# The skip term as matrix products in a fused Mamba and mixture-of-experts kernel, its gate on VectorE, and one product moved to GpSimd

## What is computed

```
xc = silu(causal_conv4(xn @ W_in[:, :512]) + conv_b)        # 512 rows x 512 channels
dt = softplus((xc @ W_x)[:, :64] @ W_dt + b_dt);  z = xn @ W_in[:, 512:]
h[l] = exp(dt[l] * A) * h[l-1] + (dt[l] * xc[l]) * B[l]     # 16 states per channel
y    = sum over the 16 states of h * C  +  D_skip * xc      # the skip term
x    = x + ga * ((y * silu(z)) @ W_out)                     # the gate, the output projection
```

## Time and profile before

| | us |
|---|---|
| median of three runs (1579.13 to 1584.12) | 1581.85 |
| the profiled execution | 1585.96 |
| its span, first to last instruction | 1584.2 |
| outside the span | 1.8 |
| first scan starts | 66.6 |
| period of a sequence in the middle (730.26 to 860.05) | 129.8 |
| end of the last scan | 1105.3 |

### The profile page before, as it was taken

One profiled execution on the slowest core, in us unless ns is written; L12 is line 12 of the kernel. 1 busy time (PEld: TensorE's weight loads), 2 busy tenths in 40 slices (PEclk: granted clock), 3 DMA queues, 4 the chain that ended last, 5 costly groups with the idle time before them and its releaser, 6 DMA issues.

```text
span 1584.2 us, 25969 instructions
## 1 busy us (share of the span) xinstructions
PE 1336.4 (84%) x7986; PEld 1086.1 (69%) x7986; DVE 1219.8 (77%) x2155; ACT 783.9 (49%) x1376; POOL 1044.8 (66%) x942
## 2 busy tenths in 40 slices
PE   3676876876867998788798798869799999999998
PEld 1254564565655776657666576768689989999997
DVE  3798999899899889989989988987355545555554
ACT  2666867767766776786787677666000000000000
POOL 2486778798889789889899878986414352122222
PEclk7787899889889889999999999999899999999999
DMA  6212121223134333244333332674967788766663
GB/s 223 74 48 77 50 54 55 75 92 88 48 100 122 123 114 126 79 143 141 104 107 104 105 111 100 180 235 136 332 179 197 209 241 221 208 194 200 198 193 85
DMA packets 129073, 216.60 MB, mean 137 GB/s; under 512 B 17805, under 2 KB 74649, under 8 KB 128809
## 3 DMA queue, kind: packets, MB, share of 16 engines
q1 hardware_dynamic: 110104, 184.12, 38.0%
q0 software_dynamic: 16064, 27.62, 7.0%
q10 hardware_dynamic: 2768, 3.21, 0.7%
HBM read 178.60 MB, written 37.22 MB: 136 GB/s over the span
## 4 chain that ended last, share of the span: by engine, by line
PE 45%; DVE 18%; POOL 14%; issue 10%; ACT 8%; DMA 3%; SPq 1%; POOLq 0%; DVEq 0%; ACTq 0%
PE psum L1665 13%; PE psum L1681 13%; POOL dBu L873 10%; DVE w_sb L1965 9%; PE psum L1477 6%; DVE y L1976 3%; PE psum L1486 2%; ACT psum L1124 2%; ACT hc L1108 2%; PE psum L1621 1%; PE psum L1466 1%; PE psum L1634 1%; DVE w_sb L1946 1%; DVE xc L1946 1%; DMA w_sb<-in_W 1%
## 5 line engine op out<-in xcount | busy, mean ns | idle before, releaser
L873 POOL TENSOR_TENSOR dBu<-w_sb,brep 128x512 f32<-128x512 f32 x512 | 645.6, 1325 | 42.1 <-issue 18.1
L1965 DVE TENSOR_TENSOR_SCAN w_sb<-psum,dBu 128x512 f32<-128x512 f32 x512 | 611.6, 1210 | 77.5 <-ACT psum L1124 54.6
L1477 PE MATMUL psum<-ident,w_sb 128*128 128x128 f32 x2048 | 316.8, 305 | 116.8 <-DVE y L1976 66.8
L1124 ACT ACTIVATE psum<-w_sb,aneg 128x512 f32<-128x512 f32 x512 | 347.4, 692 | 134.3 <-DVE w_sb L1965 131.4
L1477 PEld LDWEIGHTS psum<-ident,w_sb 128*128 128x128 f32 x2048 | 262.0, 157 | 192.5 <-DVE y L1976 106.1
L860 POOL DMA_INDIRECT out<-dBu,token x59 | 92.2, 1563 | 305.4 <-DMA out<-dBu,token 200.8
L1108 ACT ACTIVATE hc<-psum,ct 128x512 f32<-128x512 f32 x256 | 174.7, 682 | 124.8 <-PE psum L1477 96.6
L1486 PE MATMUL psum<-ident,hc 128*128 128x128 f32 x1024 | 173.7, 302 | 36.2 <-ACT hc L1108 28.8
L1486 PEld LDWEIGHTS psum<-ident,hc 128*128 128x128 f32 x1024 | 135.0, 156 | 81.9 <-ACT hc L1108 53.8
L1976 DVE SCALAR_TENSOR_TENSOR y<-psum,ct,y 128x512 f32<-128x512 f32 x240 | 174.5, 727 | 13.6 <-PE psum L1477 13.1
L1665 PE MATMUL psum<-xn,expert_pieces 128*128 128x128 f32 x928 | 111.4, 280 | 8.2 <-issue 8.2
(11 more groups left out here) (265 smaller groups left out, 1745.1 us busy)
## 6 DMA issues: line engine op xcount, KB each, us to landing
brep<-b_d SPq DMA_DIRECT2D x128, 256.0 KB, 5.4
win<-in_W SPq DMA_DIRECT2D x30, 1024.0 KB
expert_pieces<-in_W SPq DMA_DIRECT2D x29, 1024.0 KB
expert_pieces<-in_W SPq DMA_DIRECT2D x42, 512.0 KB, 5.3
dBu<-rows_d SPq DMA_DIRECT2D x35, 257.0 KB
w_sb<-in_W SPq DMA_DIRECT2D x8, 1024.0 KB
xg<-rows_d SPq DMA_DIRECT2D x22, 257.0 KB, 2.8
h_d<-hmod SPq DMA_DIRECT2D x8, 512.0 KB, 3.5
```

The lines of the kernel that those rows point to most:

```text
L873: nc.gpsimd.tensor_tensor(dBu[:, i % RING, :], u[p][:, c, :], brep[:, s % 4, :], ALU.mult).then_inc(s_dBu, 1)
L1124: nc.scalar.activation(dA[:, i % DA_RING, :], dt[p][:, c, :], ACT.Exp, scale=aneg[:, c, s:s + 1]).then_inc(s_dA, 1)
L1477: last = nc.tensor.transpose(T[:, i // DT, c * P:(c + 1) * P], hs[s % 2][:, c, i * P:(i + 1) * P], ident[:, :])
L1965: nc.vector.tensor_tensor_scan(hs[s % 2][:, c, :], dA[:, i % DA_RING, :], dBu[:, (n * UNITS + i) % RING, :], 0.0, ALU.mult, ALU.add).then_ ...
```

## The change

**The skip term.** Four 128x128 diagonal matrices of D_skip (`skip_diagonals`) are made once by VectorE in the prologue. After each `y_t`, TensorE adds 16 products of such a matrix and xc into `YT` (`add_skip`). VectorE's `o_gate` then multiplies `YT` by silu(z) in four instructions; GpSimd's `gate` is gone.

**dt times x.** The product leaves VectorE's state 13 and is made by GpSimd in four chunks after its inputs of state 15; each chunk releases its own first `dBu` of the next sequence.

**ScalarE.** In each state `decays` of unit 0 stands alone, followed by the work that stood behind unit 1 in states 0, 8, 9, 12, 13 and 14; in state 11 `softplus_in(0)` moves behind unit 2's decay, and in state 8 `o_norm` is issued in one piece ahead of unit 3's.

**The end.** The two buffers of W1 trade places, SP issues W1 of tile 12 before its rows and the rows of tiles 13, 14 and 16 after two more loads, `first(BEGIN)` is split in two around the last `add_up`, `y_t` and `add_skip`, and ScalarE applies scale and bias to the first rows of tile 13 and bias and ReLU to tile 12 in place of VectorE.

```diff
@@ -148,7 +148,7 @@
-        w1_of = [win[:, :, :], wp[:, 0:2, :]]
+        w1_of = [wp[:, 1:3, :], win[:, :, :]]
@@ -532,7 +534,7 @@
-                        if (slot_of(g) >= 3) == (t == BEGIN) and slot_of(g) != 2:
+                        if slot_of(g) in ((1, 2) if t == BEGIN else (3, 4)):
@@ -623,18 +627,20 @@
+                late_w1(BEGIN)
...
-                late_w1(BEGIN)
-                for t in (BEGIN + 1, BEGIN + 2, BEGIN + 4):
-                    late_rows(t)
...
+                for t in (BEGIN + 1, BEGIN + 2, BEGIN + 4):
+                    late_rows(t)
...
+                first_columns(BEGIN + 1)
+                sp.wait_ge(s_tr, NB * UNITS - TI)
+                all_w2(6)
...
-                all_w2(6)
@@ -715,12 +721,6 @@
-            def gate(n, p, chunks=range(CH)):
-                pool.wait_ge(s_zs, n + 1)
-                for c in chunks:
-                    pool.wait_ge(s_g, n * CH + c + 1)
-                    nc.gpsimd.tensor_tensor(gT[:, c, :], gT[:, c, :], sz[p][:, c, :], ALU.mult).then_inc(s_gate, 1)
-
@@ -860,13 +860,18 @@
 
+            def dt_x(n, p):
+                pool.wait_ge(s_dt, n)
+                for c in range(CH):
+                    nc.gpsimd.tensor_tensor(u[p][:, c, :], dt[p][:, c, :], xc[p][:, c, :], ALU.mult).then_inc(s_u, 1)
+
             def inputs(n, p, s, has_before, chunks=range(CH)):
...
                     i = n * UNITS + s * CH + c
-                    if s == 0 and has_before and c == 0:
-                        pool.wait_ge(s_u, n)
+                    if s == 0 and has_before:
+                        pool.wait_ge(s_u, (n - 1) * CH + c + 1)
                     if s == 0 and not has_before and c % 2 == 0:
@@ -937,12 +936,13 @@
+                    if has_p and s == 15:
+                        dt_x(n + 1, 1 - p)
...
-                gate(NB - 1, 1)
@@ -1204,12 +1204,21 @@
                 act.wait_ge(s_txp, t + 1)
-                act.wait_ge(s_cl[r], 48 * (t // 2) + 32)
-                act.wait_ge(s_thp, 2 * t)
+                act.wait_ge(s_cl[r], 48 * (t // 2) + (48 if t == BEGIN else 32))
+                if t == BEGIN:
+                    act.wait_ge(s_thp, 2 * t)
                 for k in range(DC):
...
                 last.then_inc(s_txt, 1)
+
+            def first_hin(t):
+                r = t % 2
+                act.wait_ge(s_thp, 2 * t + 2)
+                act.wait_ge(s_typ, t - 1)
+                for f in range(FC):
+                    last = nc.scalar.activation(hT_late[r][:, f, :], hl(t)[:, f, :], ACT.Relu, bias=cols[:, r, f:f + 1])
+                last.then_inc(s_th, 2)
 
@@ -1279,29 +1288,32 @@
-                    decays(n, p, s, (0, 1), has_o)
-                    if n in (3, 7) and s == 0:
-                        rank_in(n // 4, XB)
-                    times_c_before(n, p, s, 0, has_o)
+                    decays(n, p, s, (0,), has_o)
...
-                    if has_p and s == 1:
-                        norm(n + 1, (0, 1))
-                    if has_p and s == 3:
-                        norm_t(n + 1, 1)
...
-                    if has_p and s == 11:
-                        softplus_in(n + 1, 1 - p, 0, not has_o)
+                    if has_p and s == 12:
+                        softplus_exp(n + 1, 1 - p, 0)
+                    if has_o and s in (13, 14):
+                        o_xhat(n - 1, (2 * s - 26, 2 * s - 25))
+                    if has_o and s == 13:
+                        count_in(n - 1)
+                    decays(n, p, s, (1,), has_o)
+                    if n in (3, 7) and s == 0:
+                        rank_in(n // 4, XB)
+                    times_c_before(n, p, s, 0, has_o)
+                    if has_p and s == 1:
+                        norm(n + 1, (0, 1))
+                    if has_p and s == 3:
+                        norm_t(n + 1, 1)
...
-                    if has_o and s in (13, 14):
-                        o_xhat(n - 1, (2 * s - 26, 2 * s - 25))
@@ -1325,9 +1337,9 @@
-                        o_norm(n - 1, (0, 1))
+                        o_norm(n - 1, range(TI))
...
-                        softplus_exp(n + 1, 1 - p, 0)
+                        softplus_in(n + 1, 1 - p, 0, not has_o)
@@ -1491,15 +1501,28 @@
                 for i in range(count):
-                    nc.tensor.matmul(YT[:, DT + 1, :], zeros[:, :], ones[:, :].unsqueeze(1).to_broadcast([P, DT * 2, P]),
+                    nc.tensor.matmul(YT[:, DT + 1, :], ones[:, :], zeros[:, :].to_broadcast([P, DIN]),
                                      start=False, stop=False, skip_group_check=True)
...
                     for c in range(CH):
-                        last = nc.tensor.transpose(YT[:, i, c * P:(c + 1) * P], y[n % 2][:, i, c * P:(c + 1) * P], ident[:, :])
+                        last = nc.tensor.matmul(YT[:, i, c * P:(c + 1) * P], y[n % 2][:, i, c * P:(c + 1) * P], ident[:, :],
+                                                start=(c == 0), stop=False, is_transpose=True, skip_group_check=True)
                 last.then_inc(s_yT, 1)
+
+            def add_skip(n):
+
+                if n == 0:
+                    pe.wait_ge(s_dskd, 1)
+                pe.wait_ge(s_yT, n + 1)
+                pe.wait_ge(s_acc, 2 * NS * (n + 1))
+                for c in range(CH):
+                    for i in range(TI):
+                        last = nc.tensor.matmul(YT[:, i, c * P:(c + 1) * P], dskd[:, c, :], xc[n % 2][:, c, i * P:(i + 1) * P],
+                                                start=False, stop=True, skip_group_check=True)
+                last.then_inc(s_skip, 1)
 
@@ -1643,28 +1666,29 @@
-                    pe.wait_ge(s_g, NB * CH)
+                    pe.wait_ge(s_gate, NB * CH)
...
-            def first(t):
+            def first(t, half=None):
...
-                pe.wait_ge(s_txt, t + 1)
-                pe.wait_ge(s_w1[t % 2], 16 * (i // 2 + 1))
-                if i == 0:
-                    pe.wait_ge(s_scan, NB * UNITS)
-                elif i == 1:
-                    pe.wait_ge(s_hc, 2 * NS * NB)
-                else:
-                    pe.wait_ge(s_th, 2 * (t - 2) + 2)
-                for f in range(FC):
+                if half != 1:
+                    pe.wait_ge(s_txt, t + 1)
+                    pe.wait_ge(s_w1[t % 2], 16 * (i // 2 + 1))
+                    if i == 0:
+                        pe.wait_ge(s_scan, NB * UNITS)
+                    elif i == 1:
+                        pe.wait_ge(s_hc, 2 * NS * NB)
+                    else:
+                        pe.wait_ge(s_th, 2 * (t - 2) + 2)
+                for f in range(FC) if half is None else range(half * FC // 2, (half + 1) * FC // 2):
...
-                last.then_inc(s_thp, 2)
+                last.then_inc(s_thp, 2 if half is None else 1)
@@ -1693,6 +1717,7 @@
                     y_t(n - 1)
+                    add_skip(n - 1)
 
@@ -1797,6 +1820,8 @@
                         add_up(n, s, 0)
+                    if n == 7 and s == 15:
+                        first(BEGIN, 0)
                     if n == 7 and s == 7:
@@ -1848,6 +1873,8 @@
+                add_skip(NB - 1)
+                first(BEGIN, 1)
@@ -1976,14 +1999,14 @@
 
-            def o_skip(n, p):
-                dve.wait_ge(s_yT, n + 1)
-                dve.wait_ge(s_acc, 2 * NS * (n + 1))
+            def o_gate(n, p):
+                dve.wait_ge(s_skip, n + 1)
+                dve.wait_ge(s_zs, n + 1)
                 for c in range(CH):
...
                         return v.rearrange("p (i t) -> p i t", i=TI)
-                    nc.vector.scalar_tensor_tensor(by_tile(gT[:, c, :]), by_tile(xc[p][:, c, :]), dsk[:, c:c + 1],
-                                                   YT[:, :, c * P:(c + 1) * P], ALU.mult, ALU.add).then_inc(s_g, 1)
+                    nc.vector.tensor_tensor(by_tile(gT[:, c, :]), by_tile(sz[p][:, c, :]), YT[:, :, c * P:(c + 1) * P],
+                                            ALU.mult).then_inc(s_gate, 1)
 
@@ -2066,6 +2089,10 @@
+                dve.wait_ge(s_id, 3)
+                for c in range(CH):
+                    last = nc.vector.tensor_scalar(dskd[:, c, :], ident[:, :], dsk[:, c:c + 1], None, ALU.mult)
+                last.then_inc(s_dskd, 1)
@@ -2182,10 +2207,9 @@
-                late_xin(BEGIN + 1)
-                o_skip(NB - 1, 1)
-                late_hin(BEGIN)
+                o_gate(NB - 1, 1)
...
+                dve.wait_ge(s_th, 2 * BEGIN + 2)
```

41 lines of the change are left out of this document (15 added, 26 removed).

## The result

The changed kernel took 1586.57 us (median of 9 runs, 1584.95 to 1594.56), against 1581.85 for the kernel before in the same job (9 runs): a ratio of 1.0036, 95% interval 1.0021 to 1.0051. In a second job it was 1588.46 against 1584.66, ratio 1.0026 (1.0007 to 1.0044). So it is about 0.3% or 4 to 5 us slower, where I had forecast 2.2 us less. The time lies inside my range, and on the wrong side of no change. The profiles can't show the loss as a difference of spans: both profiled executions of the kernel before (1585.96 and, in before_again, 1587.24 us) were longer than the medians beside them, and the spans are 1584.2 and 1585.4 before, 1583.1 and 1586.2 after. The terms of the sum can be read from them all the same.

What follows compares the result with a forecast made beforehand. No engine full in the middle sequences, DVE nearest; PE in the late stage; PE's order and weights' landing between. Body +7.8 and end −10.0 gave −2.2 us: 1579.6 us against the median of 1581.85; range 1563 to 1597.

Steps and rivals of the forecast that it cites:

- Skip term: Sequences 1 to 7: o_gate waits for y_t and sixteen more products, +17.5 us in sum.
- the −5 us that I expected back: Transposes behind the skip products: with PE busy their slow run goes, 0.8 us in six sequences; bounds 0 and −6.3.
- Rival (a): add_skip in sequences 1 to 7: products run at the low clock, block 4.5 us or more, 1596 us; chance 0.20.
- The end: After the last scan: second(12) starts about 20.1 us behind it instead of 30.1; −10.0 us, bounds 0 and −12.
- PE has them just in time: After the last scan: all eight megabytes of weights land near 1122, ahead of second(12) at 1125.4.
- rival (c): After the last scan: no gain, DMAs keep PE waiting as before or ACT is late; 1589.6 us, chance 0.12.
- dt times x: Product moved to GpSimd: VectorE's saving in state 13 against later first dBu; +1.2 us, bounds −19 and +16.
- I count half of it: Sequence 3: the product on GpSimd waits behind ACT's table, comes 5.0 us late, and half is felt, +2.4 us.
- ScalarE's order: States: three waits behind ACT at tile_hin of sequences 4 to 6 go, −1.9; −1.5 us in all, bounds −9 and +9.
- the other shifts go both ways: States: ScalarE's other moved work gains and loses, +0.4 us together.
- Sequence 7: Last sequence: GpSimd loses its gates and gains no dt_x, so DVE waits less for POOL; −3 us, bounds 0 and −5.
- VectorE's two-operand rows holding up GpSimd: dt_sum beside POOL: shared SBUF port pair, one operation stands still 2 us; moving dt_x frees one meeting, sum unchanged.

Runs made afterwards that it cites:

- before_again: The kernel before, unchanged, profiled a second time: 1585.14 us, ratio 0.9988.
- skip_and_end: Changed kernel with ScalarE's order and dt times x as in the kernel before, leaving skip term, gate and new end: 1591.53 us, ratio 1.0061.
- no_products: Changed kernel with one column of one product in place of add_skip's sixteen, leaving the skip term out: 1560.16 us, ratio 0.9848.
- act_order_alone: The kernel before with ScalarE's new order in the states and nothing else of the change: 1572.10 us, ratio 0.9911.
- dtx_on_dve: Changed kernel with dt times x back on VectorE in state 13, in one instruction: 1585.09 us, ratio 0.9997.
- xin13_on_dve: Changed kernel with tile 13's scale and bias on VectorE and its columns not loaded: 1585.53 us, ratio 1.0008.
- act_order_filled: act_order_alone plus one product of zeros on TensorE behind state 9 in sequences 1 to 6: 1564.06 us, ratio 0.9876.
- filled_idle: Changed kernel plus one product of zeros on TensorE behind state 9 in sequences 1 to 6: 1582.70 us, ratio 0.9999.

## Why the prediction was wrong, step by step

I predicted −2.2 us as a sum of terms of both signs, and +4.7 and +3.8 were measured. The three largest errors are in the end, in dt times x and in ScalarE's order, and a fourth term, the clock by state, was not in the sum.

**Skip term: the place and the mechanism right, the sum partly by luck.** 18.2 us of waits for 17.5, at the place that I named. In sequence 1 I was 2.9 us too high: I took 5.44 us from a block that had run after an idle time, and the products, right behind y_t, took 3.8. In sequences 3 and 7 I was 1.7 and 0.9 too low, and these errors cancel.

Of the −5 us that I expected back, the slow transposes did go (1.04 us in all seven sequences), but the waits that DVE had behind them in the kernel before sum to 2.7 us only, 0.4 to 0.7 in sequences 2 to 6. Beside the old order of ScalarE my sum held: first to last scan, skip_and_end took 1046.6 us against 1038.7 and 1036.9 before, 8 to 10 us more, where my terms for what it contains give 17.5 − 5 − 1.4 − 3 = 8.1. Beside the new order, taking the products out gave back twice what I expected (no_products).

Rival (a), the low clock in the products, happened in one block of the sixteen in the changed kernel's two profiles: 4.66 us, over my sign of 4.5, and o_gate there waited 3.85 us. Not counted at all was a wait of DVE for PE in state 3 of sequence 3: 0.55 us before and 0.66 in act_order_alone, but 2.6 and 2.8 in the two profiles of the changed kernel, and 2.8 to 3.3 in no_products, skip_and_end and dtx_on_dve. So neither the products, nor ScalarE's order, nor dt times x makes it alone; its cause stays open.

**The end: −10 forecast, −3.8 measured** (mean of two profiles each; the old end varied by 5.6 us over four). The failed step is "PE has them just in time": second(12) began 27.6 us after the last scan, not 20.1. I reckoned the megabytes of weights at 368 GB/s and left out that small loads queue among them: of tile 13's columns, which the diff adds, the later took 12.2 us. xin13_on_dve showed that this was not all: without them W2 is late by 4.1 us, landing at 1127.6 where I had all weights near 1122, and the gain is 2.4. The DMAs had moved 372 GB/s from 1104 to 1128 there, 8.9 MB in this stretch alone: more went through the DMAs by then than my eight megabytes. It is rival (c), which I gave 0.12, in part.

**dt times x: +1.2 forecast, some +4 to +9 measured** (the two pairs with and without it). The failed step is sequence 3's: "I count half of it". The wait for ACT's table stays ahead of the product, so the whole 5 us came late, and DVE felt 3.2 and 2.4 us of it (3.2 and 2.9 in the second profile) where I had counted 2.4 in all. In the middle sequences it waited 1.4 us for POOL or nothing, and DVE's saving of 2.7 us in state 13 came back as 1.2 us of waiting for PE in state 15 and 0.5 in the next state 0. The measured range holds some of the clock's stretch too, which differs between the profiles of each pair.

**ScalarE's order: −1.5 forecast, −5.7 (undone in the changed kernel) to −11.8 (alone) measured.** The failed step is "the other shifts go both ways". I had priced one wait, of 0.63 us in state 0, and put +0.4 us for all other shifts, with no row of state 11; the scan's row there shows 2.67 us in sequences 3 to 6 of the kernel before and 3.7 in sequence 1, and moving softplus_in(0) behind unit 2's decay took 2.1 us of it. This error, in the favourable direction, hid most of the other two. How much of the −11.8 is the order and how much the clock is not separated: the kernel before with the filler alone was not run.

**Sequence 7: −3 forecast.** From first to last scan it took 126.0 and 123.8 us before, 124.7 and 124.5 after. With the 2.6 us of o_gate's wait inside, a relief of 2 to 3 us would fit, but it isn't shown: act_order_filled, with GpSimd's gates in their old place, took 121.2 us, and the wait of 0.95 us for POOL that I built on is not in before_again.

**What was missing altogether** is the stretch of states 10 to 12 at TensorE's lower level. The kernel before has it in every middle sequence for a short time; the changed kernel has it in some sequences, which then take 4.1 us more, and in others not at all. I read the clock as a mean over a sequence (0.92 before, 0.96 or 0.92 after) and never by state. By filled_idle it is worth 5 to 6 us of the changed kernel's median, about the size of the whole measured loss.

Set together from the runs: skip term and end +8.6, ScalarE's order −6 to −12, dt times x +4 to +9, against +4.7 and +3.8 measured. The parts don't add up exactly, because each moves the clock's stretch too. What sets the moment at which TensorE falls behind an idle time of 0.86 us, and why not each time, stays open.

What the prediction weighed of VectorE's two-operand rows holding up GpSimd still shows in the changed kernel where dt_sum meets GpSimd; from DVE's and POOL's timelines in sequence 4:

```profile
699.30 2.40 DVE L1978 TENSOR_TENSOR w_sb<-w_sb 128x2048 f32<-128x2048 f32 x1
```
```profile
699.21 0.31 POOL L765 TENSOR_TENSOR prod<-cnt_sb,ohs 128x64 f32<-128x64 f32 x1
699.47 2.29 POOL L767 COPY xrow<-ids 128x4 f32<-128x4 f32 x1
```

A copy of four elements, 0.18 us in the kernel before at this place, took 2.29 us, about the length of dt_sum. In the kernel before it was the product ahead of it that met dt_sum: 2.36 us at 700.27, 0.31 here. So the meeting is in both kernels, and it changed no term.

## What to carry to other kernels

Price a change of order by the waits of the engine that is in front, all of them, one row per place in a period; a wait of 2.7 us that recurs in four sequences, 3.7 in a fifth, was worth more than the feature. When independent instructions stand on one engine, the one whose input may be late goes behind those whose inputs are ready. Where a clock can fall, look at the granted clock by stage, not by period, before believing any sum of waits, and try one filler in the idle time ahead of the fall; and issue small loads that something waits for ahead of the large ones, not behind (that order was not run here; without the loads the end was 2.4 and 0.6 us shorter in two pairs of profiles).

## What the hardware showed that I had not expected

- TensorE's level in a stretch of 12 us with equal work was 1.00 in one sequence and 0.68 in the next, after the same idle time of 0.86 us; with a filler of 1.03 us there it was 1.00 in both, and the median was 5 to 6 us lower.
- The later of two loads of 1 KB each took 12.2 us behind weights at a DMA share of 1.06 (372 to 373 GB/s).
- Sixteen fp32 products of 128x128x128 took 3.84 us at full clock with a diagonal as weights, where the earlier trace rows have 3.57; what makes the difference no run shows.
